# Neighbour sums: sixty-four count products in four bursts of sixteen instead of sixteen bursts of four

## The reference

```
xn  = layernorm(x)
agg = segment_sum(xn[src], dst, 6250)             # the neighbour sums
gnn = relu(((1 + eps) * xn + agg) @ W1 + b1) @ W2 + b2
x   = x + gnn + linear_attention(xn)              # 8 heads, elu + 1, then a projection
x   = x + lstm_block(layernorm(x))                # a recurrence over 6250 cells, with
                                                  # prefix and suffix sums of gated outputs
```

## Time and profile before

| | |
|---|---|
| Time, median of 3 runs | 2192.62 us (2191.93 to 2192.69) |
| Profiled execution, span | 2193.1 us (the page has no other time of it) |
| TensorE matmuls busy | 1953.1 us, 89% of the span, 13526 of them |
| TensorE weight loads busy | 1552.2 us, 71% |
| VectorE busy | 1596.7 us, 73% |
| ScalarE busy | 1179.2 us, 54% |
| GpSimd busy | 197.6 us, 9% |
| Mean granted TensorE clock | 0.954 of full |
| Large products (line 666) | 2401 |
| Count products (line 661) | 3136 |

### The profile page before, as it was taken

One profiled execution on the slowest core, in us unless ns is written; L12 is line 12 of the kernel. 1 busy time (PEld: TensorE's weight loads), 2 busy tenths in 40 slices (PEclk: granted clock), 3 DMA queues, 4 the chain that ended last, 5 costly groups with the idle time before them and its releaser, 6 DMA issues.

```text
span 2193.1 us, 43185 instructions
## 1 busy us (share of the span) xinstructions
PE 1953.1 (89%) x13526; PEld 1552.2 (71%) x13526; DVE 1596.7 (73%) x4209; ACT 1179.2 (54%) x3147; POOL 197.6 (9%) x274
## 2 busy tenths in 40 slices
PE   5679989999999999999999989997789998899845
PEld 4567876666666666666668868886568887888833
DVE  7887878777777777777746967777876666566687
ACT  4574445555555555555533446666875665566527
POOL 3352001000000000000002200000000000000060
PEclk8799998999999999999999999999999999999975
DMA  4222330100000010010015302223553343243303
GB/s 127 89 79 83 95 97 23 32 26 26 28 29 26 25 33 26 24 33 26 24 35 174 98 39 112 112 112 130 169 150 95 124 127 109 87 130 124 114 1 117
DMA packets 96797, 170.50 MB, mean 78 GB/s; under 512 B 8213, under 2 KB 68841, under 8 KB 96384
## 3 DMA queue, kind: packets, MB, share of 16 engines
q1 hardware_dynamic: 67693, 86.80, 12.2%
q10 hardware_dynamic: 27248, 77.11, 11.4%
q0 software_dynamic: 1744, 5.21, 0.8%
HBM read 110.53 MB, written 58.56 MB: 77 GB/s over the span
## 4 chain that ended last, share of the span: by engine, by line
PE 58%; DVE 21%; ACT 11%; issue 8%; POOL 2%; DMA 1%; DVEq 0%; ACTq 0%; POOLq 0%; SPq 0%
PE psum L666 28%; PE psum L815 11%; PE psum L661 7%; PE psum L772 4%; ACT scr L1132 2%; ACT scr L1124 2%; DVE scr L1507 2%; DVE scr L1717 2%; DVE bufB L1719 1%; DVE bufB L1634 1%; DVE scr L1715 1%; ACT scr L1091 1%; PE psum L636 1%; DVE bufA L1835 1%; PE psum L610 1%
## 5 line engine op out<-in xcount | busy, mean ns | idle before, releaser
L666 PE MATMUL psum<-halves,counts 128*128 128x512 f32 x2401 | 759.3, 423 | 16.2 <-ACT counts L1029 16.2
L1532 DVE TENSOR_TENSOR wx<-rs_buf 128x392 bf16<-128x392 bf16 (+1 forms) x1568 | 545.5, 391 | 211.1 <-PE psum L661 207.2
L1029 ACT ACTIVATE counts<-psum 128x392 fp32r<-128x392 f32 x784 | 390.3, 498 | 357.3 <-PE psum L661 355.9
L815 PE MATMUL psum<-bufB,wx 128*128 128x125 f32 x3392 | 423.1, 283 | 32.5 <-DVE bufB L1719 21.5
L666 PEld LDWEIGHTS psum<-halves,counts 128*128 128x128 f32 x2401 | 393.4, 189 | 65.9 <-ACT counts L1029 21.8
L815 PEld LDWEIGHTS psum<-bufB,wx 128*128 128x128 f32 x3392 | 399.4, 194 | 56.1 <-DVE bufB L1719 37.0
L661 PEld LDWEIGHTS psum<-wx 128*128 128x128 bf16 x3136 | 170.9, 99 | 198.6 <-issue 191.8
L661 PE MATMUL psum<-wx 128*128 128x98 bf16 x3136 | 284.9, 213 | 3.7 <-DVE wx L1532 2.5
L772 PE MATMUL psum<-bufA,wx 128*128 (+1 forms) x800 | 181.7, 379 | 3.2 <-POOL rs_buf L527 3.2
L772 PEld LDWEIGHTS psum<-bufA,wx 128*128 128x128 f32 x800 | 147.9, 190 | 20.7 <-issue 3.4
L1132 ACT ACTIVATE scr<-scr 128x125 f32<-128x125 f32 x280 | 86.1, 307 | 127.5 <-DVE scr L1717 115.8
(11 more groups left out here) (265 smaller groups left out, 2519.7 us busy)
## 6 DMA issues: line engine op xcount, KB each, us to landing
bufA<-gates_of_x ACTq DMA_DIRECT2D x136, 500.0 KB, 3.4
gates_of_x<-bufB SPq DMA_DIRECT2D x24, 1000.0 KB, 3.9
x_times_eps_plus_sums<-scr SPq DMA_DIRECT2D x50, 128.0 KB, 1.7
sums_by_feature<-scr SPq DMA_DIRECT2D x50, 128.0 KB, 1.9
scr<-x_times_eps_plus_sums SPq DMA_DIRECT2D x49, 128.0 KB, 2.1
wx<-in_x_dram SPq DMA_DIRECT2D x25, 250.0 KB
x_plus_mix<-wx SPq DMA_DIRECT2D x25, 250.0 KB, 4.9
bufB<-x_plus_mix SPq DMA_DIRECT2D x25, 250.0 KB, 2.7
```

The lines of the kernel that those rows point to most:

```text
L666: return mm(psum[:, 3 + v, :], cnt[v][:, hi, :], xhl[:, hi, :, :].rearrange("p s d -> p (s d)"), start=(hi == 0), stop=(hi == NT - 1))
L815: return mm(gate_half(u, m, gate), whhv[:, k, (2 * gate + m) * P:(2 * gate + m + 1) * P], h, start=False, stop=(k == 1), skip_group_check= ...
L1029: fn(cnt[v][:, :, c * u:c * (u + 1)], psum[:, CB[u % 4], 0:PER * KEYS].rearrange("p (c h) -> p h c", h=NT), ACT.Copy).then_inc(S["c_sb"], 1)
L1532: last = tt(to, tab2[:, 0:k_, :].unsqueeze(1).broadcast_to([P, PER // 2, k_, 2]), keysT[v][:, part_, g0:g0 + PER // 2, :].unsqueeze(2).bro ...
```

## The change

TensorE's order within a tile is written anew. Ten large products (`RUN`), then four units in a row (`BURST`), four times, and then the last nine large products. The pair of transposes of keys moves from ahead of unit 4 behind 15 large products to ahead of unit 4 behind 20; the pair of turned rows from ahead of unit 10 behind 33 to ahead of unit 8 behind 30. ScalarE's copy of the turned rows moves from ahead of its unit 10 to ahead of its unit 8. The lead-in, the final tile, the ring, the banks and the streams of the other engines are as before.

```diff
--- before.py
+++ after.py
@@ -45,6 +45,7 @@
 UNITS = P // GW // PER
 STEP_UNITS = NT * UNITS
 TURNS = NT + 1
+BURST, RUN = 4, 10
 EVEN, ODD = (NT + 1) // 2, NT // 2
 RING = 8
 LGB = (6, 7, 2, 3)
@@ -687,15 +688,16 @@
                         pe.wait_ge(S["c_sb"], u0 + (UNITS * (j + 1) + len(CB)))
                         pe.wait_ge(S["row_v"], q0 + (j + 1))
                         hi = 0
-                        for u in range(UNITS):
-                            for _ in range(3):
+                        for b in range(UNITS // BURST):
+                            for _ in range(RUN):
                                 multiply(v, hi)
                                 hi += 1
-                            if j % 2 == 0 and u == 4:
+                            if j % 2 == 0 and b == 1:
                                 turn_keys(pe.snap(b0 + (1 + j // 2)))
-                            if u == 10:
+                            if b == 2:
                                 turn_rows(pe.snap(q0 + j), 1 - v)
-                            count(pe.snap(u0 + (UNITS * (j + 1) + u)), u)
+                            for u in range(b * BURST, (b + 1) * BURST):
+                                count(pe.snap(u0 + (UNITS * (j + 1) + u)), u)
                         while hi < NT:
                             last = multiply(v, hi)
                             hi += 1
@@ -1049,7 +1051,7 @@
                         for u in range(UNITS):
                             if j % 2 == 0 and u == 4:
                                 keys_out(act.snap(b0 + (1 + j // 2)), 1 - j // 2, act.snap(u0 + (1 + UNITS * j)))
-                            if u == 10:
+                            if u == 2 * BURST:
                                 rows_turned(act.snap(q0 + j), j % 2, h0 + (1 + 16 * (j // 2)))
                             count_out(act.snap(s0 + (j + 2)), act.snap(u0 + (UNITS * (j + 1) + u)), (j + 1) % 2, u)
                 for v in range(2):
```

## The result

The changed kernel takes 2113.31 us (median of 4 runs, 2111.94 to 2117.33) against 2192.27 for the kernel before (4 runs): 79.0 us less, a ratio of 0.9644 with a 95% interval of 0.9631 to 0.9656. The forecast was 2112. The profiled execution's span is 2110.1 us against 2193.1.

What follows compares the result with a forecast made beforehand. TensorE was taken to bound the neighbour-sum stretch. Switches 1.11 plus boundary 0.67 less count products 0.10 give 1.68 us a tile; 48 x 1.685 = 80.9 us off 2193.1, so 2112 us, 8 in 10 range 2098 to 2134.

Steps and rivals of the forecast that it cites:

- The bound: In the neighbour-sum stretch TensorE is the bound and stays it; VectorE needs 12.0 us a tile, ScalarE 8.4, against 14.84.
- the slack worked out: VectorE's ring has some 2.5 us of slack; ScalarE's banks come free at 2.3 of a 3.12 us cycle, 2.7 with rows.
- (a): Within a tile, eleven switches between count and large products go, at 0.101 us each: 1.11 us less.
- (c): In bursts of sixteen, the twelve count products behind the first four take 0.047 us each: +0.10 us a tile.
- Rival 3: The switch isn't paid per switch: three large products always take 0.785 us, only the boundary gives; 2160 us, chance 0.05.
- (b): At the tile's end nine large products cover ScalarE's four copies, 0.6 us to spare: 0.67 us a tile goes.
- Rival 2: A long burst is slower per count product; from 0.082 us a product the change loses; chance 0.04.
- (d): Inside a burst, the groups' waits for VectorE's tables and a free bank cost nothing.
- Rival 1: Waits come out inside the burst, no longer hidden under three large products: 2130 to 2175 us, chance 0.10.
- (e): The transposes of keys and rows move but keep their count: 0.19 us a pair, 0.29 a tile on average.
- The sum: A new loop tile takes 14.84 us, 1.685 less; 48 tiles give 80.9 us, the first counted the same.
- VectorE's wait for the count products: VectorE's idle time for the count products gets smaller by the 81 us the stretch loses, but isn't gone.

## Why the prediction was right

- **The bound.** TensorE stayed the bound: the profile shows no idle time in 692 us. VectorE's ring and ScalarE's banks kept up, with the slack worked out.
- **(a) Switches**, 0.101 each, eleven gone: with (c) taken off, 0.093 each, and 0.100 and 0.092 were measured. The number came from comparing a run of three in the loop with 25 in a row of the final tile, which was the step that carried most of the gain. Rival 3, the toll not paid per switch, is refuted by three points of a line.
- **(b) Boundary**, 0.67 less the switch that takes its place: 0.57 expected for the kernel that does it alone, 0.55 measured. The cover was right in kind and 0.2 us too careful: copies in a row come each 0.39, not 0.44. The 0.44 was a misreading of the lead-in's pair, which starts at 329.99 and 330.43. This row of the kernel before, all engines in order of time, has the second unit of that pair:

```profile
330.03 0.36 PE L661 MATMUL psum<-wx 128*128 128x98 bf16 x4 [0.17 <-DVE wx L1532]
```

The second copy begins 0.40 behind its unit, as the copy does in the loop (704.58 to 704.98): it took the pace of the units, and 0.44 says nothing of copies in a row. The error was on the safe side and left 0.8 us to spare instead of 0.6.
- **(c) Count products** in long bursts: 0.92 us for sixteen, less 0.21 for the last, is 0.047 a step, what I took. Rival 2, which lost from 0.082 on, fell. The figure of the Trainium skill, "TensorE: Matmul & The Clock Gate", section "Back-to-back issue gap" (about 81 ns for a pair with 128 columns), is not what this trace shows: 47 ns, sixteen in a row, with bf16 weights and 98 columns (61 ns for 128, as an estimate at the same time a column).
- **(d) Waits inside a burst** at nothing: 4.0 us idle before 3136 products against 3.7. Rival 1 fell, as long as a burst has no more units than there are banks.
- **(e) Transposes**: 0.22 for a pair (674.42 to 674.64), where I had 0.19; 0.04 a tile.
- **The sum**: 14.84 forecast, 14.843 measured. The first tile gave 1.0 instead of 1.685, a step at the lower clock that I had counted like the others; 0.7 us. The 48 tiles gave 79.1 + 1.0 = 80 us of the 80.9 forecast. The span fell by 83.0, with 3.5 us of luck ahead of the loop and 0.6 lost behind it; the medians fell by 79.0, and 2112 against 2113.31 is closer than the scatter outside the loop lets one forecast.
- **What was off**: VectorE's wait for the count products was to fall by 81 us and fell by 47 (207.2 to 159.8). Its line's busy time fell too, 545.5 to 497.0, as eight instructions in a row take 2.52 us (0.63 a pair) and a pair alone 0.70. When the bound gets faster by some time and the waiting engine's own work gets shorter as well, its idle time falls by the difference only.

## What to carry to other kernels

Where two kinds of matmul alternate, compare the distance between starts in a short run with that in a long one: the difference, times the switches, is what longer bursts can bring, and the busy share shows nothing of it (89% before, 90% after). A burst should be no longer than the buffers it fills (four banks here), and behind the last one there has to be as much other work as its reader takes for all of it: here 2.12 us, of which the burst itself covers 0.74 and the products behind it the rest: seven were enough, five were not. When that work is missing the wait is moved, not removed (2172.55 against 2113.31), and with a burst of twice the banks the change is a loss.

## What was not expected of the hardware

ScalarE's copies out of PSUM, 0.50 us each, follow one another at 0.39 in a row, and the only pair in the trace of before, at the start of the lead-in, couldn't show it, as its second copy followed a unit. A bf16 product of 256 columns behind a burst cost 0.04 us. And a releaser in the profile can be the wrong one when two semaphores are waited for and one of them had been given long before: a rate (0.39 against 0.62 a unit) told them apart. Left open: whether a second engine that shares the copies out of PSUM would make bursts of eight units pay; two switches, 0.20 us a tile, would be to be had, some 10 us. It was not tried.
